# A routed expert layer: gathering tiles inside the expert loop with w1 loaded per tile, and a closing layernorm in two halves

## The reference

```python
x = layernorm(x + attn(x, Wq, Wk, Wv, Wo, betas))
x = layernorm(x + ret(x, ctx, ctx, xWq, xWk, xWv))
# experts: E = 8, hidden 512, one expert per token
gate_scores = softmax(x @ Wg + bg)
top1_idx    = argmax(gate_scores)
top1_weight = gate_scores[top1_idx]
h = silu(x @ W1[top1_idx] + b1[top1_idx])
y = (h @ W2[top1_idx] + b2[top1_idx]) * top1_weight
x = layernorm(x + y)
```

## Time and profile before

| | us |
|---|---|
| median of 3 runs (898.69 to 901.77) | 899.93 |
| profiled execution | 903.15 |
| its span, first to last instruction | 901.3 |
| TensorE busy | 712.1 (79%) |
| VectorE busy | 605.1 (67%) |
| ScalarE busy | 528.7 (59%) |
| GpSimd busy | 513.4 (57%) |

### The profile page before, as it was taken

The page is one execution under the profiler, slowest core; times in us unless marked ns, Lnnn a source line. Parts: engine busy times, 40 slices in busy tenths (PEclk is TensorE's granted clock), DMA queues, the critical chain, the costliest instruction groups (busy, mean ns, idle before and its releaser), DMA issues. The chain is left out here.

```text
span 901.3 us, 26782 instructions
## 1 busy us (share of the span) xinstructions
PE 712.1 (79%) x9501; PEld 597.7 (66%) x9502; DVE 605.1 (67%) x1217; ACT 528.7 (59%) x1119; POOL 513.4 (57%) x524
## 2 busy tenths in 40 slices
PE   4789999999999999999999999748994600599920
PEld 3577788788778778778778877645664500598920
DVE  4378788788788788878878878745885510244438
ACT  3677787788788778778778878321221100477720
POOL 2167667757757756766765775633431167266742
PEclk8799999999999999999999999967996555699975
DMA  7567767767667677676776776611093011400033
GB/s 239 117 179 200 187 170 205 176 163 215 171 161 216 172 172 199 178 183 177 197 180 170 209 171 162 160 32 36 25 284 51 0 39 53 124 32 29 32 108 93
DMA packets 122154, 127.72 MB, mean 142 GB/s; under 512 B 7424, under 2 KB 101920, under 8 KB 118032
## 3 DMA queue, kind: packets, MB, share of 16 engines
q1 hardware_dynamic: 119584, 122.17, 52.8%
q0 software_dynamic: 2544, 5.21, 1.7%
HBM read 67.42 MB, written 43.16 MB: 123 GB/s over the span
## 5 line engine op out<-in xcount | busy, mean ns | idle before, releaser
L328 POOL TENSOR_TENSOR lhs<-pos_qv,ungate 64x1024 f32<-64x1024 f32 x64 | 151.7, 2370 | 161.9 <-PE mix L495 151.2
L614 ACT ACTIVATE psT<-bank 128x512 f32<-128x512 f32 x128 | 72.6, 594 | 92.5 <-PE bank L484 92.5
L766 DVE TENSOR_TENSOR lhs<-mix,zg_all 64x512 f32<-64x512 f32 x128 | 88.2, 689 | 5.8 <-PE mix L467 1.9
L353 POOL TENSOR_TENSOR e_qk<-e_qk 128x512 f32<-128x512 f32 (+2 forms) x96 | 78.6, 819 | 20.1 <-DVE e_qk L707 15.1
L484 PE MATMUL bank<-const,ps 128*128 128x128 f32 x512 | 70.0, 280 | 21.7 <-POOL ps L343 21.5
L598 ACT ACTIVATE e_qk<-e_qk 128x512 f32<-128x512 f32 x128 | 82.3, 643 | 0.0
L721 DVE TENSOR_REDUCE s_max<-bank 128x8 f32<-128x512 f32 x64 | 44.2, 691 | 48.7 <-PE bank L453 47.8
L467 PEld LDWEIGHTS mix<-pos_qv 64*64 64x64 f32 (+1 forms) x2048 | 65.6, 137 | 13.7 <-issue 11.2
L484 PEld LDWEIGHTS bank<-const,ps 128*128 128x128 f32 x512 | 55.2, 142 | 27.9 <-issue 15.7
L574 ACT ACTIVATE qk_tok<-bank 128x512 f32<-128x512 f32 x128 | 73.2, 601 | 0.0
L603 ACT ACTIVATE qkT<-bank 128x512 f32<-128x512 f32 x128 | 71.2, 610 | 1.8 <-PE bank L430 1.0
(11 more groups left out here) (212 smaller groups left out, 1694.5 us busy)
## 6 DMA issues: line engine op xcount, KB each, us to landing
scratch_qv<-qv_out SPq DMA_DIRECT2D x32, 1024.0 KB, 5.7
pos_qv<-scratch_qv SPq DMA_DIRECT2D x64, 512.0 KB, 6.6
swapT<-qkT SPq DMA_DIRECT2D x64, 256.0 KB, 4.0
zg_all<-scratch_z SPq DMA_DIRECT2D x64, 256.0 KB, 3.8
sorted_x<-padding SPq DMA_DIRECT2D x1, 2515.5 KB, 18.5
r_all<-in_x_dram SPq DMA_DIRECT2D x4, 512.0 KB, 7.0
cx<-in_ctx_dram SPq DMA_DIRECT2D x8, 256.0 KB, 2.7
w<-in_L_ffn_W_dram SPq DMA_DIRECT2D x1, 2048.0 KB, 9.7
```

What stands on the lines that cost most here:

```text
L328: pool.tensor_tensor(lhs[0:L, 1 - n, :, :], pos_qv[s, :, DK:], ungate[s, :, :], ALU.mult).then_inc(vg_ready, 1)
L353: pool.tensor_tensor(dst, e_qk[:, 0:c, DK:], e_qk[:, c:2 * c, DK:], ALU.add).then_inc(k_summed, 1)
L614: act.activation(psT[:, 4 * f:4 * f + 4, :], turn_bank[f % 2][:, :].rearrange("p (h s) -> p h s", h=4), ACT.Copy).then_inc(psT_evac, 1)
L766: dve.tensor_tensor(dst, mix[odd * DK:(odd + 1) * DK, g, :].rearrange("p (i n k) -> p i n k", n=SEG, i=4), zg_all[odd * DK:(odd + 1) * DK, ...
```

## The change

Four things are edited.

1. The padding and its store are gone, w1 isn't preloaded. Instead SyncE loads the tile's w1 from DRAM in the expert loop, to one of four buffers.
2. Nothing is scattered in the gate. SyncE stores x2 in token order (`x2_rows`), and the routing ends in a list: for each of the 39 tiles and 128 rows the token that sits there (`token_of`) and the row to which its result goes (`row_to`). The list comes from one-hot matrices multiplied on TensorE. Some of the routing is written shorter: the one-hot comes from the logits, the running sum is a scan, rounding up to whole tiles is a bit operation.
3. In the expert loop GpSimd gathers each tile's rows by `token_of` (four buffers) and scatters the results by `row_to`. ScalarE's and VectorE's copies are gone; ScalarE reads the biases in place.
4. The closing layernorm goes by halves of 16 batches; ScalarE normalises groups 0 to 5, VectorE groups 6 and 7, GpSimd adds groups 2 and 6.

```diff
@@ retention_phase: sync and gpsimd
-            sp.wait_ge(padded, 2)
-            sp.dma_start(sorted_x.rearrange("(t p) d -> p t d", p=P), padding[:, :, :]).then_inc(preloaded, 16)
-            sp.wait_ge(preloaded, 16 * (len(preload) + 1))
+            sp.wait_ge(preloaded, 16 * len(preload))
-            pool.memset(padding[:, :, :], 0.0).then_inc(padded, 1)
...
@@ gate_phase: sync
+            for g in range(NG):
+                sp.wait_ge(x2_kept, g + 1)
+                sp.dma_start(x2_rows[G * g * P:(G * g + G) * P, :].rearrange("(b p) d -> p b d", p=P),
+                             x2_row[:, G * g:G * g + G, :]).then_inc(x2_stored, 16)
@@ gate_phase: tensor
+            for b in range(B):
+                if b % G == 0:
+                    pe.wait_ge(in_row_ready, b // G + 1)
+                if b % (B // 2) == 0:
+                    pe.wait_ge(in_tile_ready, b // (B // 2) + 1)
+                    pe.wait_ge(token_ready, b // (B // 2) + 1)
+                last = pe.matmul(list_bank[:, 0:2 * NT], in_row[:, b, :], in_tile[:, b, :, :].rearrange("p o t -> p (o t)"), start=(b == 0), stop=(b == B - 1))
@@ gate_phase: scalar and gpsimd, once for each half of the batches
+                act.activation(in_tile[:, half_b, 1, :], at_tile[:, half_b, :], ACT.Copy, scale=cst("token")).then_inc(token_ready, 1)
+                pool.tensor_tensor(in_tile[:, half_b, 0, :], at_tile[:, half_b, :],
+                                   cst("batch")[:, half_b].unsqueeze(2).to_broadcast(dims), ALU.mult).then_inc(in_tile_ready, 1)
-            for b in range(B):
-                pool.indirect_dma_start(sorted_x, bass.IndirectOffsetOnAxis(ap=place[:, b:b + 1], axis=0),
-                                        x2_row[:, b, :], None).then_inc(scattered, 16)
@@ gate_phase: vector
+            dve.tensor_tensor(hot[:, :, :], logits[:, :, :], bc(top), ALU.is_equal).then_inc(done, 1)
+            dve.scalar_tensor_tensor(hot[:, :, :], hot[:, :, :], -float(E), iota, ALU.mult, ALU.add).then_inc(done, 1)
+            dve.tensor_reduce(index[:, :], hot[:, :, :], X, ALU.min).then_inc(done, 1)
+            dve.scalar_tensor_tensor(hot[:, :, :], iota, -float(E), bc(index), ALU.add, ALU.is_equal).then_inc(hot_ready, 1)
...
+            dve.tensor_tensor_scan(upto_batch[:, :, :].rearrange("p e b -> p (e b)"), cst("first"),
+                                   rank_bank[:, 1, :, :].rearrange("p e b -> p (e b)"), 0.0, ALU.mult, ALU.add).then_inc(done, 1)
...
+            for g in range(NG):
+                if g % (NG // 2) == 0:
...
+                    dve.tensor_tensor(at_tile[:, s, :], cst("tile_at").unsqueeze(1).to_broadcast(dims),
+                                      tile_u[:, s].unsqueeze(2).to_broadcast(dims), ALU.is_equal).then_inc(placed, 1)
...
+                dve.tensor_tensor(in_row[:, s, :], cst("lane").unsqueeze(1).to_broadcast([P, G, P]),
+                                  row_u[:, s].unsqueeze(2).to_broadcast([P, G, P]), ALU.is_equal).then_inc(in_row_ready, 1)
...
@@ expert_phase: sync
+            def step(t, k, i):
+                if not is_step(t, NT):
+                    e = expert_of(sp, t)
+                    if not is_step(t, 0, 1, 2, 3):
+                        sp.wait_ge(hid, 2 * (t - 3))
+                    sp.dma_start(w1_cur[k][:, :], W1[bass.ds(e, 1)].rearrange("o d h -> d (o h)")).then_inc(w1_loaded[k], 16)
@@ expert_phase: gpsimd
+            def gather(t):
+                if t < NT:
+                    if t > 3:
+                        pool.wait_ge(turned, t - 3)
+                    pool.indirect_dma_start(xs[t % 4][:, :], None, x2_rows,
+                                            bass.IndirectOffsetOnAxis(ap=token_of[:, t:t + 1], axis=0)).then_inc(x_loaded[t % 4], 16)
+            def scatter(t):
+                pool.wait_ge(y_kept, t + 1)
+                pool.indirect_dma_start(y_rows, bass.IndirectOffsetOnAxis(ap=row_to[:, t:t + 1], axis=0),
+                                        y[:, t, :], None).then_inc(stored, 16)
+            for t in range(6):
+                gather(t)
+            for t in range(NT):
+                gather(t + 6)
+                scatter(t)
@@ expert_phase: tensor
-                    turn(t + 1, 1 - p)
+                        if part == 0 and not is_step(t, NT - 1):
+                            turn(t + 1, (k + 1) % 4, i + (k + 1) // 4)
@@ finish_phase: scalar
+            for h, s in enumerate(halves):
+                norm_act(act, norm, dev_in, dev_out, s, h)
+                act.wait_ge(less_ready, h + 1)
+                for g in range(NG // 2 * h, NG // 2 * (h + 1)):
+                    if g not in by_dve:
+                        for b in range(G * g, G * g + G):
+                            last = act.activation(o[:, b, :], r_all[:, b, :], ACT.Identity, scale=norm["rstd"][:, b:b + 1],
+                                                  bias=norm["less"][:, b:b + 1])
+                        last.then_inc(o_act, 1)
```

More of the change, by code:

```diff
@@ L33 @@
 NT = B + E - 1
+WHOLE = 0xFFFFFF80
 def shape_constants():
@@ L99, in run_steps, with run_fours @@
     step(n // 2, n % 2, False, True)
+def run_fours(eng, step, n):
+    for t in range(4):
+        step(t, t, 0)
+    with eng.Fori(1, n // 4) as i:
+        for k in range(4):
+            step(4 * i + k, k, i)
+    for t in range(n - n % 4, n + 1):
+        step(t, t % 4, t // 4)
 def run_skewed(eng, step, n, skew):
@@ L1028, in _, with gate_phase @@
             residual(NG - 1)
-def gate_phase(nc, const, r_all, x2_row, stats, top, tile_expert, biases, Wg, bg, b1, sorted_x):
+def gate_phase(nc, const, r_all, x2_row, stats, top, tile_expert, token_of, row_to, biases, Wg, bg, b1, x2_rows):
     with ExitStack() as ctx:
@@ new lines, in _ @@
+            dve.tensor_tensor_scan(tile_end[:, :], cst("ones")[:, 0:E], tiles[:, :], 0.0, ALU.mult, ALU.add).then_inc(done, 1)
+            dve.wait_ge(done, 9)
+            dve.tensor_tensor(tile_start[:, :], tile_end[:, :], tiles[:, :], ALU.subtract).then_inc(done, 1)
+            dve.wait_ge(done, 10)
+            dve.tensor_tensor(row_of[:, :, :], row_of[:, :, :], tile_start[:, :].unsqueeze(2).to_broadcast([P, E, B]),
+                              ALU.add).then_inc(done, 1)
+            dve.wait_ge(done, 11)
@@ L1253, in expert_phase @@
+def expert_phase(nc, const, W1, w2, biases, tile_expert, token_of, row_to, x2_rows, y_rows):
     with ExitStack() as ctx:
@@ L1325, in turn, with step @@
                 if not is_step(t, 0, 1):
                     pe.wait_ge(xT_evac, t - 1)
-                pe.transpose(turn_bank[p][:, 0:P], x_cur[p][:, :], ident).then_inc(turned, 1)
-            turn(0, 0)
-            def step(half, p, one, two):
-                t = 2 * half + p
-                u, q = t - 1, 1 - p
+                pe.transpose(turn_bank[k % 2][:, 0:P], xs[k][:, :], cst("ident")).then_inc(turned, 1)
+            turn(0, 0, 0)
+            def step(t, k, i):
+                p, u, q = k % 2, t - 1, 1 - k % 2
+                one, two = not is_step(t, NT), not is_step(t, 0)
@@ L1402, in _, with hidden @@
-            run_steps(act, step, NT)
+            def hidden(t, p, part, e):
+                act.wait_ge(hid, 2 * t + part + 1)
+                if part == 0 and not is_step(t, 0, 1):
+                    act.wait_ge(y_done, t - 1)
+                for f in range(FT // 2 * part, FT // 2 * (part + 1)):
+                    act.activation(hT[p][:, f, :], h_bank[p][part][:, f * P:(f + 1) * P], ACT.Silu,
+                                   bias=biases[:, bass.ds(e, 1), f:f + 1].rearrange("p o d -> p (o d)")).then_inc(hid_done, 1)
@@ L1404, in _, with step, evac @@
+            def step(t, k, i):
+                if not is_step(t, NT):
+                    e = expert_of(act, t)
+                    for part in range(2):
+                        hidden(t, k % 2, part, e)
+            run_fours(act, step, NT)
         @block.vector
         def _(dve):
-            def stage_w1(t, p):
-                e = expert_of(dve, t)
+            def evac(t, p):
+                dve.wait_ge(turned, t + 1)
                 if not is_step(t, 0, 1):
                     dve.wait_ge(hid, 2 * (t - 1))
-                dve.tensor_copy(w1_cur[p][:, :], w1[:, bass.ds(e, 1), :].rearrange("p o d -> p (o d)")).then_inc(w1_staged, 1)
@@ L1448, in finish_phase @@
         y_tok = sb("y_tok", [P, B, D])
-        norm = {n: sb("o_" + n, [P, B]) for n in ("mean", "var", "dev", "rstd", "tmp")}
+        norm = {n: sb("o_" + n, [P, B]) for n in ("mean", "var", "dev", "rstd", "tmp", "less")}
         o = sb("o", [P, B, D])
```

390 lines of the change are left out of this document (156 added, 234 removed).

## The result

The changed kernel takes 891.31 us (median of 8 runs, 885.43 to 896.37) against 900.85 us for the kernel before in the same sessions (8 runs, 898.69 to 907.24): ratio 0.9888, 95% interval 0.9861 to 0.9916, so 1.1% faster. That is outside the range of 849 to 875. The profiled execution took 892.64 us, span 890.8, which is 10.5 us less than the span before.

The account below looks back on a forecast made before the run. Bounds by stage: TensorE to about 680 us, GpSimd's scatter in routing, TensorE in the experts, then VectorE. Terms -2.2-4.0-41.3+9.8-1.2 = -38.9 us gave 864.3 for the profiled execution, so 861 forecast, range 849 to 875.

Parts of the forecast that it names:

- Experts: Expert loop: a second indirect DMA per tile makes GpSimd the bound; 108.5 us against 98.7, +9.8 us.
- rival C: Expert loop: every indirect DMA pays 0.46 us of wait, 1.45 each, +11.7 us, total 873; chance 0.12.
- The prediction's own sign of being wrong: Expert loop: the forecast is wrong if the step per tile is 2.13 us or over 2.9.
- Rival B: Expert loop: gathers are hidden, TensorE still bounds, stage stays at 98.7 us plus 0.8; total 852; chance 0.16.
- the tail: End of the expert stage: from the last scatter's end to the next stage, 4.9 us.
- Rival D: Expert loop: TensorE waits at each tile and its clock stays low, stage 173 us, total 925; chance 0.04.
- Routing: First reduction to expert stage: 19.3 us instead of 60.6, -41.3 us.
- row and tile: Routing, third step: VectorE computes each token's row and tile by scan and small operations, 3.7 us.
- one-hots and listing: Routing, fourth step: one-hots on VectorE, GpSimd products and 32 TensorE matmuls, 9.7 us, ends 7 and 20.
- Start of retention: Retention's start: without the padding's memset the x1 transposes start earlier, cut by the context's arrival, -2.2 us.
- End of retention: Border to the gate: without the padding's late landing VectorE idles 0.31 us instead of 4.30, -4.0 us.
- Closing: Closing stage: layernorm by halves, normalisation shared with ScalarE, 8.9 us instead of 10.1, -1.2 us.

Follow-up runs that it names:

- E2: Changed kernel with the gathers left out after the first four tiles (output not the reference's): 849.28 us, one run.
- E5: Changed kernel with each gather after the first four replaced by a second scatter into a spare DRAM tensor (output not the reference's): 892.33 us, one run.
- E6: Changed kernel with plain DMAs of contiguous rows from GpSimd's queue instead of gathers (output not the reference's): 844.81 us, one run.
- E9: Changed kernel with a GpSimd memset of 128x640 behind every gather and scatter of the loop, DMAs 1.80 us apart: 906.91 us, one run.
- E11: Changed kernel with the padding's memset and store put back in retention and the closing stage of the kernel before: 900.23 us.
- E3: Changed kernel with w1 resident in SBUF from retention and copied by VectorE, SyncE idle in the loop: 890.81 us (4 runs), ratio to before 0.9834.
- E7: Changed kernel with all 39 gathers issued first into 39 buffers without waits, then the scatters, TensorE's loop written out: 890.99 us, one run.
- E15: E12 with each of the 32 listing matmuls incrementing the semaphore, where before only the last did: 879.96 us.
- E12: Changed kernel with x2 scattered in routing as before, x and w1 of each tile loaded by SyncE in the loop: 882.66 us (4 runs), ratio to before 0.9757.
- E13: Changed kernel with a GpSimd memset of 128x256 behind every gather and scatter of the loop, DMAs 1.48 us apart: 892.02 us, one run.
- E16: E12 with experts and closing stage in one block, SyncE itself waiting for the scatters' landing: 878.98 us (4 runs), ratio to before 0.9734.

## Why the prediction was wrong, by its steps

**Experts, +9.8 us forecast, +36.6 measured: the step that failed.** The prediction said "two are 2.54 us a tile, above 2.13: GpSimd becomes the bound". The price of an indirect DMA was right (1.28 from start to start, not the 1.45 of rival C), and so was the first y (first scatter 10.8 us after the first gather, 11.1 forecast). But from the first gather to the end of the last scatter it took 127.1 us where 103.6 were forecast, because at that spacing TensorE's increments are held until after GpSimd pauses (in the period shown they come 0.9 us after its last DMA's end). GpSimd's pauses are then forced by the missing y's, which makes the 6.5 us period: between pauses the two DMAs take 2.57 us a tile, about the forecast, and with the pauses 3.10. The prediction's own sign of being wrong, a step over 2.9, came. E2, E5, E6 and E9 show the cause in four ways: take the second indirect DMA away, replace it by another kind, by a plain one, or set both apart. Rival B assumed that only GpSimd's busy share counts; E6 and E2 are what it described, without the gathers. The other +3.2 us are the tail: 8.1 us from the last scatter's end instead of 4.9, all of it the DRAIN (6.43-3.23). I had read the tail as landing and border. Rival D priced the right place (a step of 3.6 us breaks even, 3.10 came) by the wrong cause: of the 117 us from 735.0 to the last scatter the clock read 0.50 in 10.2 and 1.00 in the rest. TensorE stood still fourteen times in that stretch, mostly for 1.8 to 2.2 us, and three of these pauses were followed by such a fall. A smaller miss is hidden under all this: I let the removal of ScalarE's and VectorE's copies give nothing, "neither was late", and with TensorE as the bound the loop runs at 1.94 and not at 2.13 (E2); whether it is the copies is not shown.

**Routing, -41.3 forecast, -39.7 measured: right in size.** Hot 2.2, the two matmuls 2.3, about as forecast; row and tile 4.0 instead of 3.7 (the scan 0.69, the low guess was 0.42; two operations on transposed views 0.62 and 0.58); one-hots and listing 10.4 instead of 9.7; to the first gather 1.9 instead of 1.4. The 9.7 was a slip: the later of its two paths, 1.4+9.0, is 10.4. That this is what came is partly luck, for the path was another: a listing matmul took 0.22 us and not 0.28, and the second 16 had to wait until 719.73 for GpSimd's second product. The one-hots took 0.88 us each for 512 columns, where 0.61 was assumed (the slope that the prediction names gives 0.68).

**Start of retention, -2.2: right** (2.4; E11 brings it back). The cut at the arrival of the context at 606.9 decided, as written. **End of retention, -4.0: right.** E3, without the padding and with w1, has the short border, as the prediction reasoned; E11 adds that w1's leaving would have done it too. **Closing, -1.2: right** as far as one trace of each shows (-1.4; -2.7 against E11, which has the old closing code). ScalarE's rows with two pointer operands:

```profile
874.84 6.26 ACT L1473 ACTIVATE o<-r_all,o_less,o_rstd 128x128 f32<-128x128 f32 x16 [1.36 <-DVE o_less L1508]
...
884.02 3.19 ACT L1473 ACTIVATE o<-r_all,o_less,o_rstd 128x128 f32<-128x128 f32 x8 [1.36 <-DVE o_less L1508]
```

Eight take 3.19 us, 0.40 each, 0.11 more than the 0.285 of the rows with one. The Trainium skill (ScalarE: Activation LUTs, "What ACT_TABLE_LOAD costs") gives 93 ns for each, an estimate of 3.0 for the eight; by that rule, the trace agrees within 0.2 us.

The sum without the experts was forecast as -48.7 and came as -47.7 (with attention's 0.6 taken out). The interval failed because every rival for the experts was a price of GpSimd's or TensorE's own work; none was a signal that comes late.

What stays open: where in the chip the increments wait, and what starts the hold. 39 gathers beside a loop of short dependent steps stop TensorE almost entirely once about nine have gone out (E7); the first ten or so of 32 scatters beside 32 matmuls that wait for nothing stop no increment (E15). The length of the row before the matmuls, the kind of DMA, the matmuls' data type, TensorE's waits between its groups and the other engines' increments differ between the two and were not separated.

## What to carry to other kernels

Before a second indirect DMA goes into a loop, look at the distance between them, not only at GpSimd's busy share. In this loop the second one cost 1.16 us a tile (3.10 against 1.94): 0.63 is GpSimd's own time, two at 2.57 us, and was to be seen in advance; 0.53 came on top because the DMAs stood under 1.5 us apart. At 1.80 apart nothing was held, but GpSimd alone took 3.60. What paid was fewer of them in the loop: put them where TensorE has nothing to signal, even if they stand exposed there (E12). And keep a block's end away from the work behind it when GpSimd has issued many: here its DRAIN grew by 0.08 us for each, and all engines waited for it.

## What the runs showed of the hardware

- TensorE's semaphore increments can be seen up to 3.8 us late in the changed kernel (4.9 in E13, 31 in E7) in a loop with indirect DMAs 1.28 to 1.48 us apart. VectorE's and ScalarE's were on time where they can be checked: VectorE's y at 749.71+0.29 is told at 750.01 and ScalarE's last half of h at 749.95+1.18 at 751.14, while GpSimd's four DMAs go out.
- GpSimd's DRAIN: 2.68, 3.23, 3.57, 6.43 us behind 32, 39, 43, 78 of its DMAs, and 6.43 too in E6 where half of the 78 were plain. Behind 39 and the two adds of the closing stage (E16) it took 4.56, and 1.36 behind the adds alone.
- The three operations beside a memset of 4.29 us ended with it in E11 again (3.78 us at L155).
